# Sorted rows of a routed feed-forward layer: 47 of 59 blocks hold 256 rows, in place of 39 blocks of 512

## The reference

```python
def _L0_ffn_ref(x, gamma, beta, Wr, br, W1, b1, W2, b2):
    E = 8
    K = 2
    ...
    xn = (x - mu) * jax.lax.rsqrt(var + EPS) * gamma + beta
    logits = jnp.einsum('bsd,de->bse', xn, Wr) + br
    top_vals, top_idx = jax.lax.top_k(logits, K)
    w = jax.nn.softmax(top_vals, axis=-1)
    ...
    for e in range(E):
        h = jax.nn.gelu(jnp.einsum('bsd,dh->bsh', xn, W1[e]) + b1[e], approximate=False)
        y_e = jnp.einsum('bsh,hd->bsd', h, W2[e]) + b2[e]
        y = y + y_e * w_full[..., e, None]
    return y
...
x = x + _L0_gnn_ref(_layernorm(x, axis=-1), adj, L0_gnn_W, L0_gnn_a)
x = x + _L0_ffn_ref(_layernorm(x, axis=-1), ...)
```

## Time and profile before

| | |
|---|---|
| time of the two runs | 1111.99 and 1113.98 us, median 1112.99 us |
| span of the profiled execution | 1111.8 us, 1.2 us under the median; it shows no other time of its own |
| busy over the whole span | PE 93%, ACT 69%, PEld 67%, DVE 61%, POOL 34% |
| mean granted TensorE clock | 0.987 |
| loads of blocks (`NMW<-sorted_x`) | 39 of 256 KB |
| stores of blocks (`sorted_y<-NMW`) | 39 of 256 KB |

### The profile page before, as it was taken

One profiled execution on the slowest core, in us unless ns is written; L12 is line 12 of the kernel. 1 busy time (PEld: TensorE's weight loads), 2 busy tenths in 40 slices (PEclk: granted clock), 3 DMA queues, 4 the chain that ended last, 5 costly groups with the idle time before them and its releaser, 6 DMA issues. The chain is left out here.

```text
span 1111.8 us, 19991 instructions
## 1 busy us (share of the span) xinstructions
PE 1035.5 (93%) x6481; PEld 744.2 (67%) x6481; DVE 678.5 (61%) x2122; ACT 766.1 (69%) x1155; POOL 383.3 (34%) x468
## 2 busy tenths in 40 slices
PE   4788789888899999799999999999999999999998
PEld 3455556555477777478888888886466666666667
DVE  4678888778544345288999999772533333333336
ACT  4998798786565554488888888885656556565561
POOL 4113778878573413446565653201000000000000
PEclk9899999899999999899999999999999999999999
DMA  8877987723246665322333232200000000000001
GB/s 290 338 273 272 385 321 294 276 96 125 81 150 228 202 192 169 106 70 83 89 89 89 86 85 74 66 30 1 1 10 11 10 18 12 11 16 14 10 15 33
DMA packets 69145, 131.15 MB, mean 118 GB/s; under 512 B 9918, under 2 KB 30764, under 8 KB 68012
## 3 DMA queue, kind: packets, MB, share of 16 engines
q1 hardware_dynamic: 60268, 111.96, 29.5%
q0 software_dynamic: 8192, 16.79, 5.0%
q10 hardware_dynamic: 576, 1.05, 0.3%
HBM read 77.60 MB, written 52.17 MB: 117 GB/s over the span
## 5 line engine op out<-in xcount | busy, mean ns | idle before, releaser
L2346 PEld LDWEIGHTS eY<-Vo,dGW 128*128 128x128 f32 x1024 | 132.4, 191 | 54.1 <-issue 52.8
L541 POOL DMA_INDIRECT sorted_x<-V,AT_I x128 | 125.5, 980 | 57.8 <-issue 37.0
L2346 PE MATMUL eY<-Vo,dGW 128*128 128x128 f32 x1024 | 134.2, 276 | 0.1
L2329 PE MATMUL eU<-XTN,V 128*128 128x512 f32 x256 | 130.9, 593 | 0.9 <-PEq L2264 0.9
L2516 DVE TENSOR_TENSOR dGW<-H,WBC 128x512 f32<-128x512 f32 x80 | 55.3, 692 | 124.9 <-PE eY L2346 124.7
L2337 PE MATMUL eU<-H,V 128*128 128x512 f32 x256 | 131.1, 594 | 0.0
L730 PE MATMUL O<-Y,HS 128*128 128x512 f32 x256 | 127.6, 618 | 0.0
L1947 POOL DMA_INDIRECT W<-sorted_y,ROW_I x96 | 96.8, 1009 | 73.4 <-PE f_T L2021 53.4
L2425 ACT ACTIVATE H<-eU,bn 128x512 f32<-128x512 f32 x128 | 99.5, 777 | 25.5 <-PE eU L2329 16.2
L2048 PEld LDWEIGHTS f_O<-f_XN,f_PT 128*128 128x128 f32 x896 | 106.8, 192 | 12.7 <-DVE X L2159 10.3
L2048 PE MATMUL f_O<-f_XN,f_PT 128*128 128x128 f32 x896 | 109.8, 276 | 2.6 <-DVE X L2159 2.0
(11 more groups left out here) (306 smaller groups left out, 2069.9 us busy)
## 6 DMA issues: line engine op xcount, KB each, us to landing
XTN<-in_adj SPq DMA_DIRECT2D x64, 512.0 KB, 7.1
masks<-NMW SPq DMA_DIRECT2D x8, 2048.0 KB
f_MK<-masks SPq DMA_DIRECT2D x60, 256.0 KB, 2.7
sorted_y<-zero SPq DMA_DIRECT2D x39, 256.0 KB
NMW<-sorted_x SPq DMA_DIRECT2D x39, 256.0 KB, 2.6
sorted_y<-NMW SPq DMA_DIRECT2D x39, 256.0 KB, 2.5
X<-in_x SPq DMA_DIRECT2D x8, 512.0 KB, 8.0
out_x<-X SPq DMA_DIRECT2D x16, 256.0 KB, 2.3
```

The costliest lines, as they stand in the source:

```text
L541: g_.indirect_dma_start(sorted_x, bass.IndirectOffsetOnAxis(ap=AT_I[b % 2][:, kt:kt + 1], axis=0), XR[b % 2][:, t * P:(t + 1) * P], None). ...
L2329: pe.matmul(U1[j % 2][:, :], V1[:, e * P:(e + 1) * P], XTN[:, b * N + q * HALF:b * N + (q + 1) * HALF], start=True, stop=True).then_inc(u1 ...
L2346: i = pe.matmul(Y[q][:, t * P:(t + 1) * P], GW[:, j % 2, t * P:(t + 1) * P], Vo[:, e * P:(e + 1) * P], start=(e == 0 and t == 0), stop=(e ...
```

## The change

The first 12 blocks stay at 512 rows. The others hold 256: (16384 / 256) + 7 - 24 = 47 of them (NR), 59 blocks in all. Rows that are computed, with those of empty places, fall from 39 x 512 = 19968 to 12 x 512 + 47 x 256 = 18176. A row of 512 in the table's first count becomes two halves, each of which is listed only where it has rows. The input buffers are cut into six of 256 rows for the small blocks, with one semaphore each, and one is free once the block six before has been turned. Turns that were counted in blocks of 512 are moved: the late loads go to every second turn from 22, `join` takes one tile in each turn from 42, and the waits of `gather` are 24 + 2t and 56 + 2t turned. The tables get 59 entries, and 36 stores of zeros clear `sorted_y`, where there were 39.

The diff, cut:

```diff
-        NB = 2 * B * N // HALF + E - 1
+        WHOLE, PART = HALF, HALF // 2
+        EARLY = 12
+        NR = 2 * B * N // PART + E - 1 - 2 * EARLY
+        NB = EARLY + NR
...
+        def tiles_of(k):
+            return (WHOLE if k < EARLY else PART) // P
...
+            XBP = part("XB").rearrange("p (k t d) -> p k t d", k=6, t=2)
...
+            def rows_in(k):
+                return XB[:, k % 3, :, :] if k < EARLY else XBP[:, (k - EARLY) % 6, :, :]
...
-            JOIN, NORM, TURN, LATE, ROWS_STEP = 27, 33, 35, 17, 2 * E + 1
+            JOIN, NORM, TURN, LATE, ROWS_STEP = 42, 53, 55, 22, 2 * E + 1
...
                 def load_block(k):
-                    if k >= 3:
+                    if k >= EARLY + 6:
+                        sp.wait_ge(turned, k - 5)
+                    elif k >= EARLY:
+                        sp.wait_ge(turned, EARLY - 2 + (k - EARLY) // 2)
+                    elif k >= 3:
                         sp.wait_ge(turned, k - 2)
                     row = sp.value_load(FROM[0:1, k:k + 1], min_val=0, max_val=SPARE)
...
-                    sp.dma_start(XB[:, k % 3, :, :], sorted_x[bass.ds(row, BLOCK), :].rearrange("(p t) d -> p t d", p=P)
-                                 ).then_inc(xb_loaded[k % 3], 16)
+                    sp.dma_start(rows_in(k), sorted_x[bass.ds(row, tiles_of(k) * P), :].rearrange("(p t) d -> p t d", p=P)
+                                 ).then_inc(rows_sem(k), 16)
...
-                    if LATE <= k < LATE + 16:
-                        late(k - LATE)
+                    if LATE <= k < LATE + 32 and (k - LATE) % 2 == 0:
+                        late((k - LATE) // 2)
...
                 for t in range(NT):
-                    pool.wait_ge(turned, 18 + t)
+                    pool.wait_ge(turned, 24 + 2 * t)
                     gather(0, t)
...
                 for t in range(NT):
-                    if 34 + t <= NB:
-                        pool.wait_ge(turned, 34 + t)
+                    if 56 + 2 * t <= NB:
+                        pool.wait_ge(turned, 56 + 2 * t)
                     gather(1, t)
...
-                    for t in range(4):
-                        j = pe.transpose(bN[k % 2][:, t * P:(t + 1) * P], XB[:, k % 3, t, :], ident[:, :])
+                    for t in range(tiles_of(k)):
+                        j = pe.transpose(bN[k % 2][:, t * P:(t + 1) * P], rows_in(k)[:, t, :], ident[:, :])
...
-                        pe.matmul(bU[c][:, :], W1E[:, q, c * P:(c + 1) * P], XT[:, q, :], start=True, stop=True
+                        pe.matmul(bU[c][:, 0:n], W1E[:, q, c * P:(c + 1) * P], XT[:, q, 0:n], start=True, stop=True
...
-                    nc.scalar.activation(GE[:, k % 2, c, :], bU[c][:, :], ACT.Gelu, bias=B1E[:, k % 2, c:c + 1]).then_inc(ge_ready, 1)
+                    n = tiles_of(k) * P
+                    nc.scalar.activation(GE[:, k % 2, c, 0:n], bU[c][:, 0:n], ACT.Gelu, bias=B1E[:, k % 2, c:c + 1]).then_inc(ge_ready, 1)
...
                 def used_blocks():
...
-                    op(v.tensor_tensor, used[:, :], got[:, :], rowno[:, :], ALU.is_gt)
-                    op(v.tensor_tensor, rest[:, :], used[:, :], taken[:, :], ALU.subtract)
-                    v.tensor_copy(ubf[:, :], rest[:, :])
+                    op(v.tensor_tensor, used2[:, 0:1], got[:, :], rowno[:, :], ALU.is_gt)
+                    op(v.tensor_scalar, got[:, :], got[:, :], -float(PART), None, ALU.add)
+                    op(v.tensor_tensor, used2[:, 1:2], got[:, :], rowno[:, :], ALU.is_gt)
+                    op(v.tensor_scalar, rest[:, :], used2[:, :], taken[:, :], None, ALU.subtract)
+                    op(v.tensor_tensor, both[:, :], rest[:, 0:1], rest[:, 1:2], ALU.add)
+                    op(v.tensor_tensor, used[:, :], used2[:, 0:1], used2[:, 1:2], ALU.add)
+                    v.tensor_copy(ubf[:, :], both[:, :])
...
-                    if JOIN <= k < JOIN + 4:
+                    if JOIN <= k < JOIN + NT:
                         if k == JOIN:
                             dve.wait_ge(early, 16 * 2 * NT)
-                        for t in (2 * (k - JOIN), 2 * (k - JOIN) + 1):
-                            join(t)
+                        join(k - JOIN)
```

More of the change, by code:

```diff
@@ L248, in program @@
         shift8, TMP = sb("shift8", [P, E]), sb("TMP", [P, B * 2 * NT])
-        BLOCK = HALF
+        BLOCK = WHOLE
         SEATS = B * N + BLOCK
@@ L362, in program, with rows_sem, rows_due @@
             xb_loaded = [sem(f"bb_xb_loaded{q}") for q in range(3)]
+            part_loaded = adj_loaded[0:6]
+            def rows_in(k):
+                return XB[:, k % 3, :, :] if k < EARLY else XBP[:, (k - EARLY) % 6, :, :]
+            def rows_sem(k):
+                return xb_loaded[k % 3] if k < EARLY else part_loaded[(k - EARLY) % 6]
+            def rows_due(k):
+                if k < EARLY:
+                    return 16 * (k // 3 + 1)
+                return 16 * (B + (k - EARLY) // 6 + 1)
             x0_step, x0_done = sem("bb_x0_step"), sem("bb_x0_done")
             X0_MEANS, X0_ROOT, X0_NORM, X0_TURNED, X0_READ = 1, 3, 5, 7, 9
-            JOIN, NORM, TURN, LATE, ROWS_STEP = 27, 33, 35, 17, 2 * E + 1
+            JOIN, NORM, TURN, LATE, ROWS_STEP = 42, 53, 55, 22, 2 * E + 1
             OTHERS, ROWS_FROM = RING + 1, RING + 1
-            assert HC == 2 and NB == 39 and NT == 8 and ROWS_FROM + E < 18 and EARLY + 16 - 4 <= 24 < JOIN and RING + E // 2 == EARLY == RING + 4
+            assert HC == 2 and NB == 59 and NT == 8 and ROWS_FROM + E < 18 and EARLY + 2 * (16 - 4) <= 36 < JOIN and RING + E // 2 == EARLY == RING + 4
+            assert JOIN + NT + 1 < NORM and TURN + 3 < NB
             block = ctx.enter_context(nc.Block(no_gpsimd_drain=True))
@@ L415, in _ @@
                             sp.dma_start(dst, src).then_inc(par_loaded, 16)
-                    clear(range((b - 2) * NB // (B - 2), (b - 1) * NB // (B - 2)))
+                    clear(range((b - 2) * CLEARED // (B - 2), (b - 1) * CLEARED // (B - 2)))
                 keep(LAST)
@@ L448, in store @@
                         sp.wait_ge(yb_stored[k % 2], 16 * (k // 2))
-                    sp.dma_start(sorted_y[bass.ds(row, BLOCK), :].rearrange("(p t) d -> p t d", p=P), YB[:, k % RING, :, :]
-                                 ).then_inc(yb_stored[k % 2], 16)
+                    sp.dma_start(sorted_y[bass.ds(row, tiles_of(k) * P), :].rearrange("(p t) d -> p t d", p=P),
+                                 YB[:, k % RING, 0:tiles_of(k), :]).then_inc(yb_stored[k % 2], 16)
                 def late(n):
@@ L798, in result @@
                     for c in range(HC):
-                        for t in range(4):
+                        for t in range(tiles):
                             j = pe.matmul(bY[q][:, t * P:(t + 1) * P], GE[:, q, c, t * P:(t + 1) * P], W2E[:, q, c * P:(c + 1) * P],
-                                          start=(c == 0 and t == 0), stop=(c == HC - 1 and t == 3))
+                                          start=(c == 0 and t == 0), stop=(c == HC - 1 and t == tiles - 1))
                     j.then_inc(out_ready, 1)
                 def work(k):
-                    q = k % 2
+                    q, n = k % 2, tiles_of(k) * P
                     pe.wait_ge(xt_ready, k + 1)
@@ L834, in list_blocks @@
                     pe.wait_ge(table_step, TAKEN + 3)
-                    pe.matmul(TC[0:1, 0:NB], rel[:, :], hot[:, :], start=True, stop=True)
+                    pe.matmul(TC[0:1, 0:NB], rel[:, :], hot[:, :], start=True, stop=False)
+                    pe.matmul(TC[0:1, EARLY:NB], part_rows[:, :], hot2[:, :], start=False, stop=True)
                     pe.matmul(TC[0:1, NB:2 * NB], ef[:, :], hot[:, :], start=True, stop=True)
-                    pe.matmul(TC[0:1, 2 * NB:3 * NB], dest[:, :], hot[:, :], start=True, stop=True)
+                    pe.matmul(TC[0:1, 2 * NB:3 * NB], dest[:, :], hot[:, :], start=True, stop=False)
+                    pe.matmul(TC[0:1, 2 * NB + EARLY:3 * NB], part_rows[:, :], hot2[:, :], start=False, stop=True)
                     pe.matmul(TC[0:1, 3 * NB:4 * NB], full[:, :], hot[:, :], start=True, stop=True)
                     pe.matmul(TC[0:1, 4 * NB:5 * NB], minus1[:, :], hot[:, :], start=True, stop=True)
-                    pe.matmul(TC[0:1, 5 * NB:5 * NB + 2], rest[:, :], within[:, :], start=True, stop=True
+                    pe.matmul(TC[0:1, 5 * NB:5 * NB + 2], both[:, :], within[:, :], start=True, stop=True
                               ).then_inc(table_step, 1)
@@ L1447, in _ @@
                         result_rows(k - ROWS_FROM)
-                    if JOIN <= k < JOIN + 4:
+                    if JOIN <= k < JOIN + NT:
                         if k == JOIN:
                             dve.wait_ge(early, 16 * 2 * NT)
-                        for t in (2 * (k - JOIN), 2 * (k - JOIN) + 1):
-                            join(t)
-                    if JOIN + 1 <= k < JOIN + 5:
```

(7 more changed lines are left out.)

43 lines of the change are left out of this document (25 added, 18 removed).

## The result

The changed kernel takes 1153.76 us (median of 1152.95 and 1154.57) against 1112.99 before: the ratio is 1.0372, with a 95% interval of 1.0353 to 1.0391. It is slower by 40.8 us. The forecast was 57 us, and its range 1154 to 1182 us: the side and the cause were right, the size was not, and the time lies at the lower edge of the range. The profiled execution's span is 1151.2 us, 39.4 above the 1111.8 of before, at the same mean clock of 0.987.

The account below looks back on a forecast made before the run. SP's instructions were to bind the small blocks: 58 blocks turned at 497.2 us, plus 17.6 us of gathers, ends stage two at 514.8, 57.0 us later than before; 1170 us, slower by 5%, range 1154 to 1182.

Parts of the forecast that it names:

- SP becomes the bound: Stage two, small blocks: SP's 3.10 us a turn exceeds the engines' 2.1 us, so SP is behind by 1 us each turn.
- SP's turn of 3.10 us: Stage two: halved bytes leave SP's turn at 3.10 us, 3.6 with a late load; 41 turns make 127.1 us.
- the other two terms: SP, blocks 16 to 57: 16 late loads at 0.5 us, 8.0 us; occasional long issues, 2.4 us.
- the table: Before block 16: seven more VectorE instructions for the table delay SP's path by 0.4 us, bounds 0 to 1.4.
- (a): Rival, stage two: SP's turn shrinks and the engines' 2.1 us rules; 1114 us, no change; chance 0.08.
- (b): Rival, stage two: SP's turn is shorter, 2.6 us, but still rules; 1150 us; chance 0.07.
- The tail: End of stage two: 14 GpSimd gathers, 17.6 us, follow 58 turned blocks; the next stage waits until 514.8 us.
- rival (c): End of stage two: GpSimd's gathers are hidden and SP's end at 504 rules, 11 us less; 1159 us; chance 0.05.
- rival (d): Stage two: idling TensorE stays at 1.2 GHz, 3.94 us a small block, 24 us on top; 1194 us; chance 0.05.
- The engines' 2.1 us: Stage two: TensorE's L813, a gelu, a copy and hand-overs let the engines do a small block in about 2.1 us.

Follow-up runs that it names:

- e1: Changed kernel without SP's register load of NEED from block 16 on, one wait on a constant instead: 1129.16 us, ratio 1.0136 to the kernel before.
- e3: Changed kernel with one more, unused register load on SP in each turn from block 16 on: 1179.32 us, one run.
- e4: Kernel before without the register load of NEED from block 16 on, one wait on a constant instead: 1113.63 us, ratio 0.9995.
- e5: Kernel before, with SP moving only half of each block's rows in and out from block 12 on: 1111.55 us, one run.
- e10: Changed kernel with loads from block 16 on and stores of the small blocks both doubled to 512 rows: 1165.25 us, ratio 1.0462 to the kernel before.
- e2: Changed kernel with GpSimd waiting for its gathers to land before the engines meet at the end of stage two: 1165.21 us, one run.
- e7: Changed kernel without NEED loads from block 16, late loads issued by ScalarE, rows of four blocks per register load: 1119.75 us, ratio 1.0058 to before.
- e8: e7 with four extra stores of blocks 12 to 15 spread over later blocks and batch 1's gathers started earlier: 1113.80 us, ratio 0.9994 to before.
- e9: Changed kernel with loads from block 16 on doubled to 512 rows, stores unchanged: 1157.31 us, ratio 1.0393 to the kernel before.

## Why the prediction was right in its cause and wrong in its size

**SP becomes the bound: right.** No waits of SP in 129 us, TensorE idle for a quarter of the time behind the landing of `sorted_x`, and e1 and e3 show it by experiment. e4 shows the other half of the step, that this cost lay under TensorE before.

**SP's turn of 3.10 us: mis-sized.** "Nothing in the rows goes by bytes ... So the turn stays at 3.10 us" was the sentence that failed. It measured 2.86 where nothing else falls into the turn. The issue of a load did stay at 0.35 us, as I had argued, but the register loads around it didn't: two of them with their waits went from 1.63 to 1.38 us. e5 finds that length in the kernel before as soon as its transfers are halved, and e10 finds the old one again, in part of the turns, when they are doubled. From the load of block 16 to that of block 57 I had put 127.1 + 8.0 + 2.4 = 137.5 us; the changed kernel took 129.8. The shorter turn alone takes off 41 x 0.24 = 9.8 us, and the other two terms, 10.4 us in the forecast, came to 12.6. One reason is a reading: 3.10 and 3.61 were among the shortest turns of their kind in the kernel before, where the 16 turns with a late load average 3.84 us, almost without a wait of SP. That e10, with the bytes of before, took 137.4 us is therefore close by some luck: its 25 plain turns average 3.05 us and its 16 with a late load 3.82, one below and one above what I had put. Block 16 came at 356.22 (356.7 forecast); the table was written only 0.2 us later than before. So of the 17.6 us by which the forecast of the span missed, 8.1 lie ahead of the load of block 57 (at 486.05, not at 494.2), and nearly all the rest is the next step.

I had named this possibility, as the rivals (a) and (b), and put only 0.15 on them. The argument against them was SP's list of waits. That list proves that SP waited for no semaphore; it does not prove that an instruction costs the same beside smaller transfers. (In (a) the 27 blocks were put at 108 us; at 3.94 us each they are 106, so some 8 us were to be won there, not 9.)

**The tail: a wrong step.** "All engines meet, GpSimd's issues included, so the next stage ... now begins after 514.8." The gathers themselves went as forecast, 14 of them at 1.26 us, 17.5 us from 488.88 to 506.42. But the meeting does not wait for them to run: it waited for SP's last store, at 497.38, and GpSimd went on 0.44 us later with seven gathers still to start. This was rival (c), to which I had given 0.05, and it is worth the other 9 us: 506.4 - 497.4. e2 gives the tail the meaning that the prediction gave it, with one landing on top, and it costs 11.5 us. The rows of before could not tell the two apart, since SP's last store, the last gather and VectorE's last result all ended within 1 us there. Both misses, 8 and 9 us, point the same way; that the time still touched the range is no merit of the sum.

**TensorE's clock, rival (d): it did not stay down.** TensorE idled a quarter of the time, in pieces of a microsecond or so before each block's transposes, where I had said a third. Its clock fell twice, as the windows of 360 to 365 and 465 to 475 show, and came back. The turn that began in the first fall took 3.36 us on TensorE (from one L840 at 359.76 to the next at 363.12), while SP's loads went on at 2.87 and 2.86 us (359.08, 361.95, 364.81): a passing fall was made good, as the argument against (d) had it.

**The engines' 2.1 us**, an estimate, was near: 2.15 in e7, though a gelu and a copy of 256 columns take 0.47 and 0.56 us in the changed kernel and not the 0.40 each that went into it. **Rival (a)**, no change, is what e8 reaches, with SP's work taken away by hand and not by itself.

The Trainium skill, "DMA: Bandwidth & Descriptors", section "Latency and other measured facts", puts a register load at 600 ns or more. What e1 took away and e3 added, a register load with its short instructions, comes to 0.61 and 0.55 us a turn, near that figure; the trace's records of the loads alone, 0.27 to 0.31 us on average in the changed kernel, are about half of it. By the page's price three loads and two issues made 2.5 us, and the measured 2.86 lies between that and my 3.10.

## What to carry to other kernels

A loop has costs that go by rows and costs that go by turns. Before blocks are made smaller, add up what the queue engine does in a turn (register loads, waits, issues), although the page shows it no busy time, and set it against the new turn of the busiest engine. An empty list of waits says that a queue is the next bound, but not that its instructions will cost the same when the transfers around them change. And at a meeting of engines, ask whether an engine has to have run its queue or only to have handed it on.

## What the runs showed of the hardware

A register load on SP can cost more while larger transfers are under way. Over the last 27 to 30 of them the trace's records of the loads of NEED average 0.49 us in the kernel before (256 KB loads and stores), 0.33 with half the bytes there (e5), 0.28 in the changed kernel (128 KB), 0.33 with its loads doubled (e9) and 0.45 with loads and stores doubled (e10). For FROM it is 0.41, 0.36, 0.31, 0.32 and 0.35. The load of TO, which comes right behind the issue of a block's load, is 0.27 to 0.28 in all five.

One instruction can bring the rows of four blocks into registers: in e7 its record is 0.30 us in the median, against 0.27 for one row of TO in the changed kernel.
